# A wait for one PSUM bank instead of two, and products of zeros, in the attentions of a long fp32 kernel

## What is computed

```
q, k, v = split(x @ W + b)                  # 16 heads of 8
s = softmax(q @ k.T * 8 ** -0.5 [+ causal mask])
x = x + (s @ v) @ W_p + b_p
```

## Time and profile before

| | |
|---|---|
| median of three runs | 6210.3 us |
| the profiled execution's own time | 6186.59 us |
| its span, first to last instruction | 6183.6 us |
| busy: TensorE | 5438.7 us (88%) |
| busy: VectorE | 4344.0 us (70%) |
| busy: ScalarE | 4103.8 us (66%) |
| busy: GpSimd | 2675.8 us (43%) |
| mean granted TensorE clock | 0.935 |

### The profile page before, as it was taken

The page is one execution under the profiler, slowest core; times in us unless marked ns, Lnnn a source line. Parts: engine busy times, 40 slices in busy tenths (PEclk is TensorE's granted clock), DMA queues, the critical chain, the costliest instruction groups (busy, mean ns, idle before and its releaser), DMA issues. The chain is left out here.

```text
span 6183.6 us, 154170 instructions
## 1 busy us (share of the span) xinstructions
PE 5438.7 (88%) x57386; PEld 3859.9 (62%) x57386; DVE 4344.0 (70%) x6705; ACT 4103.8 (66%) x7765; POOL 2675.8 (43%) x2406
## 2 busy tenths in 40 slices
PE   6777887599999999999999577699999999999997
PEld 2223332287777777777777222477777777777775
DVE  7876544577777767777775588677777777777774
ACT  5773552377777677777676377577777777777774
POOL 1101100265555555555554111456555555555552
PEclk8996776699999999999999699899999999999998
DMA  0000000000000000000000000000000000000000
GB/s 12 1 1 5 1 1 8 26 14 18 17 22 17 22 15 19 18 17 21 19 19 13 7 1 1 29 19 16 19 18 18 22 18 20 16 20 18 18 21 17
DMA packets 173242, 93.21 MB, mean 15 GB/s; under 512 B 81044, under 2 KB 169392, under 8 KB 172464
## 3 DMA queue, kind: packets, MB, share of 16 engines
q1 hardware_dynamic: 172464, 82.87, 5.0%
HBM read 68.80 MB, written 1.05 MB: 11 GB/s over the span
## 5 line engine op out<-in xcount | busy, mean ns | idle before, releaser
L1638 POOL TENSOR_TENSOR cross<-raw,tab_b 128x512 f32<-128x512 f32 x768 | 990.3, 1314 | 300.8 <-ACT raw L1508 299.0
L724 DVE TENSOR_REDUCE arena<-PS 128x1 f32<-128x512 f32 (+3 forms) x1408 | 856.3, 650 | 288.3 <-PE PS L548 168.7
L675 ACT ACTIVATE arena<-PS 128x1024 f32<-128x1024 f32 (+1 forms) x704 | 676.0, 969 | 354.7 <-PE PS L571 252.7
L1644 POOL CAST kT_b<-kT 128x512 bf16<-128x512 f32 x384 | 273.6, 713 | 1285.1 <-ACT kT L1562 1285.1
L1731 DVE TENSOR_TENSOR oT<-PS,rec_den 128x288 f32<-128x288 f32 (+1 forms) x768 | 327.1, 426 | 648.2 <-ACT rec_den L1542 648.2
L1702 DVE TENSOR_TENSOR rot<-PS,tab_a 128x512 f32<-128x512 f32 x768 | 524.3, 687 | 276.9 <-PE PS L1387 156.2
L1508 ACT COPY raw<-PS 128x512 f32<-128x512 f32 x768 | 448.8, 590 | 328.2 <-PE PS L1387 287.4
L1356 PE MATMUL PS<-qT,kT 64*128 64x96 f32 x8448 | 661.3, 287 | 0.0
L1534 ACT ACTIVATE PT<-PS 128x576 f32<-128x576 f32 (+1 forms) x768 | 469.1, 611 | 257.4 <-PE PS L1356 245.7
L548 PE MATMUL PS<-k_parts,q_parts 32*128 32x512 f32 (+3 forms) x1408 | 378.1, 525 | 275.6 <-DVE arena L724 263.3
L1718 DVE TENSOR_TENSOR rot<-rot,cross 128x1024 f32<-128x1024 f32 x384 | 609.3, 1587 | 8.6 <-POOL cross L1638 7.8
(11 more groups left out here) (239 smaller groups left out, 12910.2 us busy)
## 6 DMA issues: line engine op xcount, KB each, us to landing
w_qk<-in_w_pairs SPq DMA_DIRECT2D x196, 128.0 KB, 2.1
w_v<-in_w_pairs SPq DMA_DIRECT2D x100, 128.0 KB, 2.2
w_o<-in_w_out_pairs SPq DMA_DIRECT2D x192, 64.0 KB, 1.9
xs<-x_tok SPq DMA_DIRECT2D x24, 256.0 KB
xs<-x_tok SPq DMA_DIRECT2D x24, 254.0 KB
w<-in_L_ffn_W SPq DMA_DIRECT2D x12, 341.0 KB
q_parts<-max_rows SPq DMA_DIRECT2D x192, 2.0 KB
raw<-in_c_E SPq DMA_DIRECT2D x2, 896.0 KB, 4.7
```

What stands on the lines that cost most here:

```text
L675: nc.scalar.activation(PT[u % 4].rearrange("p (a n) -> p a n", a=2)[:, :, first_q:512], PS[:, 2 * (u % 2):2 * (u % 2) + 2, first_q:512], A ...
L724: nc.vector.tensor_reduce(maxima[:, 2 * m + h, qt, kh:kh + 1], bank[:, 0:keys_of(qt, kh)], AX.X, ALU.max).then_inc(bank_free, 1)
L1638: nc.gpsimd.tensor_tensor(dst[:, :, :, o:o + 32], src[:, :, :, other:other + 32], tab[:, :, o:o + 32].unsqueeze(2).broadcast_to([128, 8, 2 ...
```

## The change

In all three attentions `maximum` now makes one head's maximum at a time and waits for that bank alone, and the loop issues maximum 0, the scores, maximum 1. The masks of both maxima stay behind maximum 1. In the causal attention `values` first issues, in every step with kt > 0, two matmuls of a 128x128 bf16 tile of zeros with itself repeated four times (512 columns) that add to the whole of bank 6; kt = 0, each half's first step, has none. The tile is one more cut of the arena and is cleared by GpSimd at the start of an attention.

```diff
@@ attend
         rden = cut(16)
+        nothing = cut(64).bitcast(BF16)
@@ GpSimd
                     nc.gpsimd.memset(spread[n].rearrange("p g (h r) -> p (g h) r", h=4)[:, :, 0:8], 0.0).then_inc(preset, 1)
+                nc.gpsimd.memset(nothing, 0.0)
@@ TensorE
-                def maximum(g, couple):
+                def maximum(g, couple, h):
                     qt, kh, m = couple
                     pieces = 4 if qt >= 4 else 2 + kh
-                    need(pe, made_first if g == 0 else made, pieces if g == 0 else (g - 1) * 4 + pieces)
+                    if h == 0:
+                        need(pe, made_first if g == 0 else made, pieces if g == 0 else (g - 1) * 4 + pieces)
                     keys, masked = keys_of(qt, kh), causal and kh == qt // 4
                     q, k = operand["q"][g % 3], operand["k"][g % 3]
-                    banks = [bank_for("max", g, couple, h) for h in range(2)]
-                    for h in range(2):
-                        r = slice(32 * (2 * m + h), 32 * (2 * m + h) + 32)
-                        last = nc.tensor.matmul(banks[h][:, 0:keys], q[r, 128 * qt:128 * qt + 128], k[r, 512 * kh:512 * kh + keys],
-                                                start=True, stop=not masked, tile_position=(32 * (2 * m + h), 0), skip_group_check=True)
-                        if not masked:
-                            last.then_inc(full, 1)
+                    bank = bank_for("max", g, couple, h)
+                    r = slice(32 * (2 * m + h), 32 * (2 * m + h) + 32)
+                    last = nc.tensor.matmul(bank[:, 0:keys], q[r, 128 * qt:128 * qt + 128], k[r, 512 * kh:512 * kh + keys],
+                                            start=True, stop=not masked, tile_position=(32 * (2 * m + h), 0), skip_group_check=True)
+                    if not masked:
+                        last.then_inc(full, 1)
@@ values
                     if t % STEPS == 0:
                         pe.wait_ge(vb_ready, i + 1)
+                    if causal and kt > 0:
+                        for _ in range(2):
+                            nc.tensor.matmul(PS[:, 6, :].rearrange("p (a n) -> p a n", a=4), nothing, nothing.unsqueeze(1).broadcast_to([128, 4, 128]),
+                                             start=False, stop=False, skip_group_check=True)
@@ TensorE's loop
                         if couple:
-                            maximum(g, couple)
+                            maximum(g, couple, 0)
                         if 0 <= t < ALL:
                             scores(2 * t + slot)
+                        if couple:
+                            maximum(g, couple, 1)
                         if couple:
                             mask_maximum(g, couple)
```

## The result

The changed kernel takes 6124.8 us, the median of four runs (6115.3 to 6142.0), against 6210.6 us before (6206.4 to 6220.3): a ratio of 0.9863, 95% interval 0.9837 to 0.9888, 86 us. The forecast was 6208 us in a range from 6174 to 6246. The change is much faster than forecast, and the rest of this document finds out which of its two edits did it.

A forecast was written before the change was run, and what follows sets the result against it. It saw a closed loop of VectorE and TensorE bounding the first and last attention, and TensorE with a swinging clock the causal one. Terms -9.9 - 1 + 8.2 = -2.7 us, carried to the median 6210.3, gave 6208 us, range 6174 to 6246.

The forecast's parts named there:

- Warm-ups: Pipeline start of the three attentions: 0.34 us waits go, 9.9 us gained in first and last, 1 us in causal.
- The steady loop: First and last attention: the 2.81 us loop between VectorE and TensorE stays as it is, zero gain.
- start of maximum 1: Leg of the loop in first and last attention, from the first reduction's end to maximum 1: 0.16 us.
- The causal attention: Own bank in its steps: no gain, since most maxima are masked and both masks still come behind maximum 1.
- 0.18 us x 256 steps = 46 us of gain: First and last attention: gain if the cover went and steps shrank to VectorE's work; zero was taken instead.
- The zeros: Causal steps: 80 pairs ahead of values, each 0.45 us at full clock, 0.90 at half, 0.05 beside narrowest values.
- The clock's new pattern: Causal groups: full clock from step 6 to step 3 of the next group, which then takes 46.3 us.
- early falls: Causal groups where the clock falls early all the same: 7 us each, half of one counted, +3.5 us.
- Full clock throughout: Rival: zeros carry the causal clock over each half's first step too, groups of 42.6 us, total 6177; chance 0.19.
- The zeros do lift the clock: Denies the rival that the causal clock keeps its pattern despite the zeros, total 6244; chance 0.21.
- VectorE didn't become the bound: Denies the rival of 2.63 instead of 2.81 us a step in the unmasked attentions, total 6162; chance 0.07.
- The lone maximum didn't break the packing: Denies the rival that each late slot's separate maximum 1 takes its 0.21 us alone, total 6262; chance 0.06.

The follow-up runs named there:

- the split: The change's first edit alone (own bank per maximum, scores between the maxima, no products of zeros) on the kernel before: 6114.2 us, ratio 0.9865.
- the extra wait: The split without zeros, plus one wait, satisfied since the start, ahead of each maximum 1: 6153.3 us in its only execution.
- zeros only: The kernel before with the products of zeros alone added: 6164.1 us, ratio 0.9939.
- fewer waits: The kernel before, leaving out TensorE's wait for the pieces of q and k where it is already met: ratio 0.9987.

## Why the prediction was wrong

**Warm-ups: right in kind, too small.** "30 x 0.33 = 9.9 us" and 1 us for the causal one. From the first piece to the first values, the first attention went from 50.7 to 44.5 us, the last from 51.6 to 44.5 and the causal one from 57.2 to 52.7: 17.8 us. The forecast's 15 pauses in each are there. Up to the row maxima the first attention's 32 reductions took 19.2 us instead of 25.2 (32.92 to 52.1 and 32.73 to 57.9), and behind them only 0.2 us was gained. Some 4.4 us of these 6.0 are thirteen waits of 0.34 (two more come later); the rest is that reductions without a wait between them follow each other every 0.60 us, where a pair by itself takes 1.29. The forecast left VectorE's work at 1.29 a pair. In the causal warm-up the pauses ahead of masked maxima also got some 0.09 us shorter each, which was not counted.

**The steady loop: this step failed first.** "In the steady loop I expect nothing", and it named every leg correctly. The legs stayed; the one of 0.16 us, "start of maximum 1", was taken as a constant. It depends on what is waited for: 0.75 instead of 0.84 us after the reduction's start once maximum 1 has one wait of its own (two waits: 0.83). That is 0.10 us a step together with the next leg (0.42 instead of 0.44), and the values' stretches of the two unmasked attentions fell from 391.6 to 383.3 and from 392.1 to 386.0 us. The forecast's own test, "I am wrong if the steady step moves by more than 0.05 us", caught it.

**The causal attention, "nothing there either": this was the costly one.** The split alone took 48 us out of it: some 9 by shorter steps, 3 in the warm-up, and about 35, within the 11 us named above, by the clock. The forecast asked of the zeros only what they would do to the clock, and never of the split. Yet it had read that the clock fell where TensorE had done little; an edit that packs the same work into less time could act on that as well as one that adds work. The runs bear that out: the extra wait lengthens the step by 0.06 us, adds no work, and shows a clock of 0.78 over the causal values instead of 0.87, more than the 0.05 between two profiles with equal steps (0.73 and 0.68). The bound "0.18 us x 256 steps = 46 us of gain" was set for the other attentions alone, and a chance of 0.07 given to it.

**The zeros: priced right.** A pair "0.45 us at full clock": 0.44 measured. In steps with the narrowest values a pair was to be hidden, 0.05 us: in the changed kernel the two intervals around step 11 take 5.34 us, in split only 5.27, so 0.07. Around step 3 it was not hidden: in group 2, at full clock in both, the two intervals take 6.79 and 6.48 us, so 0.31. The array's change of shape added 0.10 us at most, as the row said, and not the 0.23 that was worked out beside the rule.

**The clock's new pattern: right in four of six groups.** Full clock until step 3 or 4, one fall, back by step 6, since the first step of a half gets no zeros: that is what the changed kernel shows in groups 1, 3, 4 and 5, while groups 2 and 6 held full clock throughout. The group was to take 46.3 us and takes 42.8. The split gave 1.6 us of that: zeros only, with the same single fall, takes 44.4 in the same group. The other 1.9 were missed with the zeros: the fall that the forecast took from the kernel before lasted 10.2 us (728.5 to 738.7), the one in zeros only 6.8 (769.4 to 776.2). By groups the causal values gained 18.7 us in groups 1 to 5 (the forecast had a gain of 0.8 and 3.5 against it for early falls) and 11.3 in group 6 (3 was forecast), which held full clock throughout.

**The sum.** -17.8 for -10.9 in the warm-ups, -14.4 for 0 in the unmasked values, -23.1 for +8.2 in the causal values: -55.3 for -2.7, in the profiled executions. Of the remaining 31 us to the medians' 86, 24 are there because the profiled execution of before was that much under its median, and 3 because that of after was over. Where the 24 lay can't be said of executions without a profile. The profile of fewer waits, 20 us longer than that of before, has 11 of them in the causal attention and 7 in the window layers, so a good part of the 86 may be clock in the causal attention too.

**The rivals.** None came near: the two faster ones said 6177 and 6162. Full clock throughout was wrong in kind, as the clock still fell in most groups. The zeros do lift the clock (0.73 to 0.93 on their own). VectorE didn't become the bound in the plain step: TensorE still stands in the loop. The lone maximum didn't break the packing.

## What to carry to other kernels

A loop between two engines has a leg for the start after a release, and that leg is something to edit: here it paid to put the wait that comes last on an instruction with no other wait, or at least not behind the others. And where the granted clock swings, price every edit twice, once by its own time and once by what it does to TensorE's work per microsecond; here, with the split in place, fillings were worth their time at the steps around which the clock fell and not everywhere, and they were cheapest behind products that already used the whole array.

## What the runs showed of the hardware

- One wait more, long since met, on a matmul that waits for a bank: 0.83 instead of 0.75 us from the start of the reduction that frees the bank. A third one adds nothing (0.84). With three waits of which the one met last stands second, it is 0.80.
- A product on the whole array between products in 32-row tiles costs 0.32 us beyond its columns; between the mask on the whole array and values in 32-column tiles a pair costs 0.10 us beyond them.
- VectorE's four reductions of 128x512 take 2.48 us in the split's plain step, where their banks are filled one by one, and 2.63 before, where they are filled two and two; back to back in the warm-up 16 take 9.65, 0.60 each, though a single one is listed with 0.68.
- With the same matmuls, TensorE's clock over the causal values goes with the length of the step: 0.68 and 0.73 of full clock with a plain step of 2.81 us, 0.76 and 0.78 with 2.76, 0.87 with 2.70, each from one profile.
- Products of zeros lift the granted clock: 0.93 instead of 0.73 over the causal values when they alone are added.
